# Early statistics of a four-layer convolution kernel: two of VectorE's channels moved from layer 3 into layer 2

## The reference

```
x = x + conv_L0(gn(x))   # per-sample depthwise 3x3, weights made from the channel means
x = x + conv_L1(gn(x))   # dense 3x3, 32 to 32 channels, on signs of input and weights
x = x + conv_L2(gn(x))   # as layer 0
x = x + conv_L3(gn(x))   # as layer 0
# gn: 16 groups of 2 channels, mean and variance over a group and the whole image
# conv_L0/2/3: pooled = mean(gn); hidden = relu(pooled @ w1 + b1)
#              taps = (hidden @ w2 + b2), 9 for each channel of each sample
```

## Time and profile before

| | |
|---|---|
| median of 3 runs | 4206.77 us (4196.08 to 4215.0) |
| profiled execution | 4186.62 us, span 4184.8 us |
| TensorE matmuls busy | 3237.2 us, 77% of the span |
| VectorE busy | 2121.7 us, 51% |
| ScalarE busy | 1696.0 us, 41% |
| POOL busy | 1964.2 us, 47% |
| mean granted TensorE clock | 0.912 |
| SP's DMA queue (q1) | 311104 packets, 467.67 MB |
| ScalarE's DMA queue (q10) | 251142 packets, 359.81 MB |
| moved in all | 846.05 MB, mean 202 GB/s |

### The profile page before, as it was taken

How to read it: one execution, slowest core, us unless ns; L and a number is a source line. 1 busy time by engine, 2 the same in 40 slices (tenths; PEclk the granted TensorE clock), 3 DMA queues, 4 the chain that set the end, 5 groups by cost and what they waited for, 6 DMA issues and landing times.

```text
span 4184.8 us, 70829 instructions
## 1 busy us (share of the span) xinstructions
PE 3237.2 (77%) x26592; PEld 2057.9 (49%) x26592; DVE 2121.7 (51%) x6310; ACT 1696.0 (41%) x2466; POOL 1964.2 (47%) x3175
## 2 busy tenths in 40 slices
PE   0676998769886698867986788965988768887698
PEld 0453655435564455544555445643555535455355
DVE  1626854277432774328643385424854257542672
ACT  2442733336243363434533354333633426334233
POOL 1326544265442655336552564516644175452754
PEclk9997999889998899988998989988999889998899
DMA  6279788887979789697896978959789697897846
GB/s 219 55 128 195 189 290 249 147 182 194 302 210 169 170 215 305 177 199 170 236 305 138 214 169 256 309 99 214 183 252 293 110 207 174 256 294 122 190 74 227
DMA packets 611739, 846.05 MB, mean 202 GB/s; under 512 B 492227, under 2 KB 492998, under 8 KB 578630
## 3 DMA queue, kind: packets, MB, share of 16 engines
q1 hardware_dynamic: 311104, 467.67, 49.3%
q10 hardware_dynamic: 251142, 359.81, 28.8%
q0 software_dynamic: 49152, 14.05, 2.0%
HBM read 452.84 MB, written 267.45 MB: 172 GB/s over the span
## 4 chain that ended last, share of the span: by engine, by line
PE 53%; DMA 16%; DVE 10%; issue 5%; ACT 5%; POOL 4%; ACTq 4%; SPq 3%; DVEq 0%; POOLq 0%
PE acc L1028 29%; PE acc L1045 17%; DMA signs<-arena 6%; POOL y L546 4%; DMA dense_out<-arena 4%; DMA arena<-signs 4%; PE acc L1107 3%; DVE dense_stats L907 2%; ACTq L641 2%; ACT arena L634 2%; ACTq L571 2%; ACT arena L619 2%; SPq L426 2%; DMA arena<-dense_out 2%; DMA arena<-x 1%
## 5 line engine op out<-in xcount | busy, mean ns | idle before, releaser
L1028 PE MATMUL acc<-y,arena 64*128 64x384 f32 x9216 | 1683.5, 492 | 40.1 <-ACT y L603 24.8
L1028 PEld LDWEIGHTS acc<-y,arena 64*128 64x128 f32 x9216 | 986.9, 190 | 589.5 <-ACT y L603 109.1
L603 ACT ACTIVATE y<-acc 128x768 f32<-128x768 f32 x896 | 697.5, 808 | 1256.9 <-PE acc L1045 1256.2
L1045 PE MATMUL acc<-arena 64*128 64x384 f32 x4608 | 968.6, 514 | 221.3 <-issue 198.7
L525 POOL TENSOR_SCALAR arena<-arena,cst,fill 128x24 f32<-128x24 f32 (+1 forms) x1536 | 620.5, 424 | 913.7 <-issue 622.5
L546 POOL TENSOR_TENSOR y<-arena,y 128x3072 f32<-128x3072 f16 x88 | 529.9, 6045 | 738.8 <-DMA arena<-dense_out 738.8
L907 DVE BATCH_NORM_STATS2 dense_stats<-y 128x6 f32<-128x192 f32 x1536 | 408.1, 345 | 726.4 <-POOL y L546 726.1
L1045 PEld LDWEIGHTS acc<-arena 64*128 64x128 f32 x4608 | 519.9, 196 | 460.2 <-issue 239.0
L344 POOL DMA_DIRECT2D arena<-y x1024 | 529.2, 524 | 399.9 <-PE acc L1045 327.0
L1107 PE MATMUL acc<-arena,wd_side 128*32 128x384 fp8e4 (+1 forms) x10752 | 471.0, 330 | 288.6 <-DMA arena<-signs 231.8
L1107 PEld LDWEIGHTS acc<-arena,wd_side 128*32 128x32 fp8e4 x10752 | 307.3, 101 | 473.7 <-issue 243.7
(11 more groups left out here) (88 smaller groups left out, 1344.5 us busy)
## 6 DMA issues: line engine op xcount, KB each, us to landing
out<-y ACTq DMA_DIRECT2D x128, 1152.0 KB, 13.7
y<-x ACTq DMA_DIRECT2D x112, 1152.0 KB, 35.0
arena<-x SPq DMA_DIRECT2D x147, 576.0 KB, 6.9
dense_out<-arena ACTq DMA_DIRECT2D x384, 192.0 KB, 7.0
arena<-dense_out SPq DMA_DIRECT2D x192, 384.0 KB, 6.9
arena<-y SPq DMA_DIRECT2D x512, 141.0 KB
arena<-signs SPq DMA_DIRECT2D x192, 250.0 KB, 10.3
signs<-arena SPq DMA_DIRECT2D x128, 312.5 KB, 3.5
```

The costliest lines, as they stand in the source:

```text
L603: nc.scalar.activation(y[:, 2 * g:2 * g + 2, k * KN:(k + 1) * KN], acc[:, 2 * k:2 * k + 2, 0:KN], ACT.Identity, accum_out=sums[:, g, k:k + ...
L1028: nc.tensor.matmul(acc[:, 2 * k + odd, 0:KN], w_center[at, slot, 2 * q + odd, :], y[at, 2 * g + odd, k * KN:(k + 1) * KN], start=turn == 0 ...
L1045: nc.tensor.matmul(acc[:, 2 * k + odd, 0:KN], w_halo[at, slot, q, :], halo[at, bt % HALO_SLOTS, q, k * KN:(k + 1) * KN], start=False, stop ...
```

## The change

Two lists of pairs and one list of channels change, and SP's loop of layer 2 is written for the new number. VectorE makes six statistics in layer 2 (pairs 1, 3, 5, 7, 9, 11) in place of four (pairs 2, 6, 9, 13), and six in layer 3 (pairs 0, 1, 2, 4, 5, 6) in place of eight (also 8 and 9). The number of channels and what is computed stay the same.

```diff
-AHEAD_WITH = [2, 6, 9, 13]
+AHEAD_WITH = [1, 3, 5, 7, 9, 11]
 AHEAD_DVE = [(AHEAD_FIRST + PAIRS + n, 2) for n in range(len(AHEAD_WITH))]
-AHEAD_LATE = [(AHEAD_FIRST + PAIRS + len(AHEAD_WITH) + n, (0, 2, 1)[n % 3]) for n in range(8)]
+AHEAD_LATE = [(AHEAD_FIRST + PAIRS + len(AHEAD_WITH) + n, (0, 2, 1)[n % 3]) for n in range(6)]
-LATE_WITH = [0, 1, 2, 4, 5, 6, 8, 9]
+LATE_WITH = [0, 1, 2, 4, 5, 6]
...
                     if b < BATCHES - 1:
                         load_ahead(sp, s, AHEAD_ACT[2 * b + 2])
-                    if b in (1, 3, 5):
-                        load_ahead(sp, s, AHEAD_DVE[b // 2 + 1])
+                    if b + 1 < len(AHEAD_DVE):
+                        load_ahead(sp, s, AHEAD_DVE[b + 1])
                     halos(first + b + HALO_SLOTS)
```

## The result

| | before | changed |
|---|---|---|
| median, 20 runs each | 4200.87 us (4178.34 to 4215.0) | 4215.54 us (4191.34 to 4242.1) |
| ratio | | 1.0044, 95% interval 1.0026 to 1.0062 |
| profiled execution, span | 4184.8 us | 4189.5 us |

The change makes the kernel slower by 0.44%, about 18 us (11 to 26). The forecast was -3 us. A trace is one execution: that of the changed kernel is the shortest of its 20 runs, that of e1 the shortest of its 12, those of e2 and e14 the longest of theirs, so the ratios decide what a kernel costs and the traces say where.

A forecast was written before the change was run, and what follows sets the result against it. TensorE was taken to bound layer 2, DMA the stretch from layer 3 into the next layer 0. 4186.6 + 18 (layer 2) - 21 (layer 3) = 4183.6 us profiled, -3; forecast median 4204 us, range 4174 to 4238.

The forecast's parts named there:

- The layer-3 term: Layer 3: removing two 576 KB loads a sample was to gain 3 us a sample, -21 us in all.
- The DMA engines have room (share 0.76): Layer 2: TensorE paces it, busy 97.48 of 101 us, and DMA has room; no charge for added bytes.
- The wait on SP behind VectorE, +18: Layer 2: SP's wait for VectorE delays halos and ScalarE's odd load; 2.6 us a sample, +18 us in seven.
- w - 1.2 us: Layer 2: cost to the pace taken for a ScalarE wait of w us for its ahead load, the rest absorbed.
- 1.18 MB at 300 GB/s is 3.9 us ... so I take 3 us, -21: Layer 3: bytes of two removed loads become time, at most 27.5 us over seven samples; -21 taken.
- A stall of 7 us costs 1 us net: Layer 3 to dense layer: samples with the pair-10 stall average 270.2 us, without 269.2, so losing it gains little.
- Layer 2 hangs on TensorE, the stretch on DMA: Bound: engine time in layer 2 (97.48 of 101 us), DMA from layer 3 into next layer 0 (share to 0.99).
- VectorE's work is free: Layer 2's added statistics (2.08 us each) cost TensorE nothing; layer 3's removed ones are worth nothing, VectorE idling there.
- Sum: Whole kernel: 4186.6 + 18 - 21 = 4183.6 us for the profiled execution, -3 us; forecast median 4204.
- relief rival: Layer 3's pair-10 stalls stay gone (-32), layer 2 absorbs most later issue (+5); 4180 us, chance 0.27.
- blocked rival: Layer 2, rounds 0 to 4: late third-slot loads hold up halos and ScalarE's loads; +32 net, 4239 us, chance 0.27.
- POOL's clearing: Layer 3: 2.2-us stage clearing moves ahead of chunk 6's border, hidden by POOL's idle time; otherwise +15 us.

The follow-up runs named there:

- e1: Kernel before with only the layer-3 half: six late statistics instead of eight, two channels left out, layer 2 as before; ratio 0.9982 (0.9959 to 1.0004).
- e2: Kernel before with only the layer-2 half: six statistics there, still eight in layer 3, two channels taken twice; ratio 1.0070 (1.0043 to 1.0096).
- e14: Kernel before taken the opposite way: three statistics in layer 2, nine in layer 3; ratio 1.0011 (0.9989 to 1.0033).
- e12: Kernel before with six unblocked slot-2 loads in layer 2, rounds 0 to 5, eight late ones, VectorE's work there unchanged; ratio 1.0048 (1.0022 to 1.0073).
- e6: Kernel before with three late statistics in layer 3 instead of eight, five channels left out; ratio 0.9978 (0.9945 to 1.0012).
- e13: Kernel before with two more VectorE statistics in layer 2, taken from SBUF, no load added; ratio 0.9988 (0.9967 to 1.0009).
- e17: Changed kernel with statistics at even pairs and layer 2's slot-2 loads after the first issued by ScalarE; ratio 1.0298 (1.0266 to 1.0331) to the kernel before.

## Why the prediction was wrong

The step that failed is in layer 2: the forecast charged the two added loads only for the place where SP waits and put their own cost at nothing. The layer-3 term was too large besides.

- **"The DMA engines have room (share 0.76)"**: this is the step that failed. Six loads in successive rounds, with no wait on SP and no additional work on VectorE, cost +20 us (9 to 31, e12), and nothing in the sum stood for that.
- **The wait on SP behind VectorE, +18**: the mechanism is there, the size was not. The first wait of ScalarE is 2.82 us for a predicted 2.9, and the round-0 halos start 2.5 us after VectorE's statistics begin, as worked out. At round 1 the wait was 0.92 us in the first sample and not 2.5, and in round 2, where I had VectorE no longer late, SP still stood for it (451.74 against 449.71, 2.0 us) and ScalarE waited 1.3 us and more at pair 7 in every sample. In time it is some 6 us, with an error of 9. That the whole half measured +29 (18 to 40), with my +18 just at its edge, is in part luck: a wait priced too high stood in for loads that were not priced.
- **Its price**: the rule "w - 1.2 us" fits the first two of its rows and gives 2.4 us for the third, where the row has 4.1. Its upper bound of +50 is not what its own terms give, 2 x 4.1 - 2.2 = 6.0 us a sample, +42, as the rival has it.
- **"1.18 MB at 300 GB/s is 3.9 us ... so I take 3 us, -21"**: the term was mis-sized. Measured alone it is -8 us (-17 to +2, e1), by the other pairs -11 and -17, by the traces 2 us a sample, -14. The pair-10 stalls went in every sample and pair 8's stayed (5.8 to 9.0 us), as predicted, but chunk 5 came only 3.5 us sooner after pair 8, and bytes don't turn into time at 300 GB/s there (e6: 3.1 us for 9.8). The stretch to the dense layer was to be 3 us shorter; in the changed kernel it is 1.0 (268.8 for 269.8), in e1 2.4. "A stall of 7 us costs 1 us net" rested on means of four and three samples, 1.0 apart, in groups that reach from 267.6 to 273.4, and on stalls of 5.4 us in the mean; the direction was right, the figure was no evidence.
- **Layer 2 hangs on TensorE, the stretch on DMA**: right for layer 2 as far as it is undisturbed (87.1 us); for the stretch only half, since time freed in it mostly came back as a later stall.
- **VectorE's work is free**: right in layer 2 (e13). In layer 3 no run parts it from the loads.
- **Sum**: both terms erred the same way, by about 11 us in layer 2 (+29 for +18) and 4 to 13 in layer 3. Neither the relief rival (-32 kept) nor the blocked rival in its full form came in: waits over 3 us stand in two of the seven samples. The blocked rival had the sign.
- **POOL's clearing** moved without effect, as said: in the changed kernel TensorE has no stall at pair 12.

Open: how the 20 us of the loads divide between their number and their rounds, the share of the wait on SP (6 us with an error of 9), and why more samples of layer 2 are disturbed with six loads, beyond the DMA share.

## What to carry to other kernels

Where a loop's own progress triggers its transfers, take a stall away and ask when the next transfers start, before counting the gain. Price a moved load at both ends with what lands just in time beside it, not with the mean share of the stage, and don't take a share of 0.8 for room: here it was not. In a queue served in order, a load that waits for a slow engine should stand behind what others need, in a round where its wait is already met.

## What was not expected of the hardware

- With the slot-2 loads on ScalarE's idle queue and in the middle of the round, SP's own 576 KB loads took 9.4 us to land where they had taken 6.1, and a kernel with the same bytes became 3% slower (e17).
- Leaving 2.95 MB a sample out of a stretch whose DMA share is 0.99 in its later part (640 to 700 us) shortened it by 3.1 us, a third of what 300 GB/s gives (e6).
- Two loads more a sample in layer 2, at a share of 0.77 to 0.90 in the rounds of before, cost 20 us in seven samples (9 to 31) with no work attached to them (e12).
